# A transformer block on one core: the last gate exponential moved behind the last gelu, and the last tile finished in two halves

## The reference

```python
x = x + attn(layernorm(x))            # 16 heads of 8, causal, with ALiBi slopes
z = layernorm(x)
logits = rms(z @ gate_w.T + gate_b) * rms_w          # 8 experts
g = max(softmax(logits / 0.5));  norm_g = g / (g + 1e-6)
h = gelu(z @ w1[e] + b1[e])           # every expert e, 256 hidden features each
y = sum over e of (h @ w2[e] + b2[e])
out = x + y * norm_g
```

## Time and profile before

| | us |
|---|---|
| median of 3 runs | 312.45 (312.29 to 312.54) |
| the profiled execution | 311.52 |
| its span, first to last instruction | 309.8 |
| PE busy | 283.4 (91%) |
| DVE busy | 206.7 (67%) |
| ACT busy | 187.2 (60%) |
| POOL busy | 90.3 (29%) |

### The profile page before, as it was taken

The page is one execution under the profiler, slowest core; times in us unless marked ns, Lnnn a source line. Parts: engine busy times, 40 slices in busy tenths (PEclk is TensorE's granted clock), DMA queues, the critical chain, the costliest instruction groups (busy, mean ns, idle before and its releaser), DMA issues.

```text
span 309.8 us, 5270 instructions
## 1 busy us (share of the span) xinstructions
PE 283.4 (91%) x1643; PEld 181.9 (59%) x1643; DVE 206.7 (67%) x831; ACT 187.2 (60%) x290; POOL 90.3 (29%) x212
## 2 busy tenths in 40 slices
PE   8527899999779999999999999999999999989993
PEld 3413665655547666757566576666566655647871
DVE  5878668787877767565777784648776821367871
ACT  6480066746539376958467296857397796525462
POOL 1449200713133246021431164020400333500250
PEclk9955789999999999999999999999999999999998
DMA  7441005230300023004000141011001000000101
GB/s 203 160 121 45 4 2 201 51 112 17 108 2 2 0 55 115 0 8 114 0 6 0 38 120 44 2 41 47 3 2 38 0 3 2 0 1 2 34 0 34
DMA packets 12811, 13.47 MB, mean 43 GB/s; under 512 B 2224, under 2 KB 9264, under 8 KB 12528
## 3 DMA queue, kind: packets, MB, share of 16 engines
q1 hardware_dynamic: 11596, 11.89, 12.4%
q0 software_dynamic: 1024, 1.05, 1.6%
q10 hardware_dynamic: 164, 0.21, 0.3%
HBM read 5.40 MB, written 1.05 MB: 21 GB/s over the span
## 4 chain that ended last, share of the span: by engine, by line
PE 61%; DVE 25%; POOL 5%; issue 4%; ACT 2%; DMA 1%; DVEq 0%; POOLq 0%; ACTq 0%
DVE unused L1189 14%; PE ffn_bank L933 11%; PE pv_bank L865 8%; PE v_ring L809 8%; PE a_ring L831 8%; PE a_ring L754 5%; PE a_ring L755 4%; PE a_ring L756 4%; PE a_ring L843 3%; POOL var L375 1%; PE v_ring L816 1%; DVE z L1087 1%; PE v_ring L894 1%; PE v_ring L878 1%; POOL var L376 1%
## 5 line engine op out<-in xcount | busy, mean ns | idle before, releaser
L1189 DVE CUSTOM_DVE_ANT_0 unused<-v_ring,cst 128x256 bf16<-128x256 f32 (+3 forms) x256 | 111.4, 488 | 44.2 <-PE v_ring L809 39.8
L620 ACT ACTIVATE probs<-a_ring 128x512 f32<-128x512 f32 x160 | 86.9, 599 | 70.2 <-PE a_ring L843 40.9
L809 PE MATMUL v_ring<-k_stack,q_stack 128*128 128x512 f32 (+1 forms) x176 | 82.2, 506 | 3.6 <-DVE row_max L1189 1.8
L831 PE MATMUL a_ring<-q_stack,k_stack 128*128 128x512 f32 (+3 forms) x256 | 63.3, 329 | 0.3 <-ACT probs L620 0.3
L638 ACT ACTIVATE hidden<-a_ring,cols_sb 128x512 f32<-128x512 f32 x64 | 43.1, 689 | 27.8 <-PE a_ring L756 27.7
L831 PEld LDWEIGHTS a_ring<-q_stack,k_stack 128*128 128x128 f32 x256 | 45.1, 192 | 13.3 <-issue 5.5
L933 PE MATMUL ffn_bank<-hidden,w_sb 128*128 128x512 f32 x100 | 51.4, 599 | 0.9 <-ACT hidden L638 0.9
L809 PEld LDWEIGHTS v_ring<-k_stack,q_stack 128*128 128x128 f32 x176 | 34.1, 200 | 25.4 <-issue 11.4
L865 PE MATMUL pv_bank<-probs,v_ones 128*32 128x256 f32 (+3 forms) x512 | 42.4, 440 | 0.0
L539 POOL TENSOR_SCALAR_AFFINE_SELECT probs<-probs 128x512 f32<-128x512 f32 x16 | 10.1, 634 | 105.9 <-ACT probs L620 105.9
L754 PE MATMUL a_ring<-zT_hi,w_hi 128*128 128x512 f32 x64 | 28.2, 441 | 0.8 <-DVEq L1073 0.8
(11 more groups left out here) (130 smaller groups left out, 340.6 us busy)
## 6 DMA issues: line engine op xcount, KB each, us to landing
k_stack<-k_hi SPq DMA_DIRECT2D x60, 32.0 KB
q_stack<-q_hi SPq DMA_DIRECT2D x6, 256.0 KB
hidden<-w SPq DMA_DIRECT2D x1, 1024.0 KB, 7.5
k_stack<-k_lo POOLq DMA_DIRECT2D x32, 32.0 KB, 2.1
x_res<-x SPq DMA_DIRECT2D x4, 256.0 KB, 2.8
w_sb<-w SPq DMA_DIRECT2D x1, 1024.0 KB, 7.1
out<-result SPq DMA_DIRECT2D x4, 256.0 KB, 2.2
x_in<-x SPq DMA_DIRECT2D x3, 256.0 KB, 3.1
```

What stands on the lines that cost most here:

```text
L620: act.activation(probs[:, n % 2, quads[0]:quads[-1] + 1, KIND_AT[kind]:KIND_AT[kind] + cols], a_bank()[:, 0:len(quads) * cols].rearrange(" ...
L809: pe.matmul(dst, q_stack[b % 2][:, s, n * P:(n + 1) * P], k_stack[:, s, quads[0]:quads[-1] + 1, 0:cols], start=True, stop=True).then_inc(v ...
L831: last = pe.matmul(dst[:, at:at + P * (TB - j)], k_stack[:, s, q, j * P:(j + 1) * P], q_stack[b % 2][:, s, j * P:T], start=(at == 0), stop ...
L1189: ins = dve.tensor_tensor_reduce(unused[:, (uses[0] - 1) % V_BANKS, at:at + cols], bank_[:, at:at + cols], cst[:, C_MASK + T - cols:C_MASK ...
```

## The change

Three things are done, all in the last batch's end.

The gate's exponential moves on ACT from behind gelu 13 to behind gelu 15. The evacuation of `ffn_bank` is two activations of 128 x 256, each with its own `ffn_evacuated` increment; PE transposes two 128-token tiles after each and puts the halves in two banks of `v_ring`; DVE gates two tiles of each half and raises `result_ready` on the second instruction itself, with no `settle` and no `v_freed`; SP issues a store of 128 KB for each half, and waits for five stores in all instead of four.

```diff
@@ sync
             store(B - 2)
-            store(B - 1)
-            sp.wait_ge(stored, 16 * B)
+            for h in range(2):
+                tiles = slice(h * TB // 2, (h + 1) * TB // 2)
+                sp.wait_ge(result_ready, B + h)
+                sp.dma_start(out_view[B - 1][:, tiles, :], result[:, tiles, :]).then_inc(stored, 16)
+            sp.wait_ge(stored, 16 * (B + 1))
@@ scalar
                 gelu_tile(B - 1, m)
                 if m == 1:
                     evacuate_ffn(B - 2)
-                if m == NT - 3:
-                    gate_exponentials(B - 1)
-            evacuate_ffn(B - 1)
+            gate_exponentials(B - 1)
+            act.wait_ge(ffn2_done, NT * B)
+            act.wait_ge(result_ready, B - 1)
+            for h in range(2):
+                cols = slice(h * T // 2, (h + 1) * T // 2)
+                act.activation(ffn_T[:, cols], ffn_bank[:, cols], ACT.Identity,
+                               bias=b2_sum[:, 0:1]).then_inc(ffn_evacuated, 1)
@@ tensor
-            transpose_ffn(B - 1)
+            for h in range(2):
+                pe.wait_ge(ffn_evacuated, B + h)
+                dst = v_bank()
+                for n in range(h * TB // 2, (h + 1) * TB // 2):
+                    last = pe.transpose(dst[:, n * P:(n + 1) * P], ffn_T[:, n * P:(n + 1) * P], ident)
+                last.then_inc(v_filled, 1)
@@ vector
             route(B - 1)
             take_gates(B - 1)
-            take_ffn(B - 1)
+            dve.wait_ge(stored, 16 * (B - 1))
+            for h in range(2):
+                bank_ = v_bank()
+                for n in range(h * TB // 2, (h + 1) * TB // 2):
+                    ins = dve.scalar_tensor_tensor(out=result[:, n, :], in0=bank_[:, n * P:(n + 1) * P],
+                                                   scalar=gate[(B - 1) % 2][:, n:n + 1], in1=x2[(B - 1) % 2][:, n, :],
+                                                   op0=ALU.mult, op1=ALU.add)
+                ins.then_inc(result_ready, 1)
```

## The result

| | median us | lowest to highest | runs |
|---|---|---|---|
| before | 312.45 | 311.29 to 312.67 | 9 |
| after | 310.18 | 309.08 to 311.36 | 9 |

The ratio is 0.9933, with a 95% interval from 0.9914 to 0.9953: between 1.5 and 2.7 us faster, 2.27 by the medians.

The account below looks back on a forecast made before the run. It took ACT's queue, by the exponential placed in it, to bound the point before the last plain tiles. Gains 1.22 + 0.50 + 0.10 + 0.38 = 2.20 us took the median from 312.45 to 310.25, range 309.8 to 311.3.

Parts of the forecast that it names:

- end of ffn2, from the last split pass: PE's last plain tiles: with the exponential behind gelu 15, ffn2 ends at 303.17 instead of 304.39, gain 1.22.
- ffn2's end to DVE's start: Evacuation and transposes in halves: DVE starts 1.01 behind ffn2 instead of 1.51, gain 0.50.
- DVE's end to SP's last issue: Signal to SP: DVE's instruction raises the semaphore itself, so SP follows 0.07 later instead of 0.17, gain 0.10.
- issue to landing: Last store: half the packets, 1.80 from issue to landing instead of 2.18, gain 0.38.
- the unbroken 1.88: PE's two plain tiles take 1.88 coming straight from other matmuls, not 2.00 with a restart (gain then 1.10).
- The cover: On ACT before the evacuation: 0.86 us left after table load and exponential; without cover the whole 1.5 us on the path.
- The 0.44: A half evacuation on ACT takes 0.44 us, by 0.95 ns a column; bounds 0.34 and 0.68.
- Rival 1: Last stores: the halved store gives nothing back; gain 1.8 or 1.7, time 310.65 to 310.75; chance 0.18.
- Rival 2: ACT becomes the bound before the evacuation: a 2.66 us switch, time 310.85, or another table load, 310.7; chance 0.08.
- Rival 3: TensorE's granted clock falls to 1.2 GHz in the tail: time 312.25, or 313.65 if earlier; chance 0.07.
- Rival 4: Gelu 14 on ACT is held by something else, a bank or ring slot: gain 1.0, time 311.45; chance 0.04.

Follow-up runs that it names:

- e1: Move only, on the kernel before: the exponential behind gelu 15, the end on the whole tile as before; median 310.94 us, ratio to before 0.9953.
- e4: The kernel after with a one-column gelu that nobody reads behind the exponential, bringing one more table load before the evacuation; median 310.63 us.
- e6: The kernel after with evacuation, transposes and gating in four pieces of 128 tokens, each in its own bank, and two stores of 128 KB; median 309.94 us.
- e3: The kernel after with the last tile stored in one piece of 256 KB once both halves are gated; median 310.30 us.
- e7: As e6 (the kernel after in quarters), but with three stores, two by SP and one by ACT's queue, the last of 64 KB; median 310.04 us.
- e5: The kernel after with tiles 14 and 15 of the last batch split by DVE too, `route` ahead of tile 15's split; median 309.49 us.
- e10: The kernel after with 20 unread 128 x 512 bf16 matmuls in PE's idle stretch after batch 0's projections; median 310.10 us, ratio 0.9918.

## Why the prediction was right

It said 310.25 and the runs gave 310.18. Part of that nearness is luck, since the runs of one kernel lie 2.3 us apart: for the profiled execution the same sum said 309.3, and it took 310.28. 0.87 us of that miss lie ahead of the tail. With them taken off, ffn2 ends at 304.06 - 0.87 = 303.19, where the prediction said 303.17. The steps are checked in the tail, each from the rows above.

| step | predicted gain | measured |
|---|---|---|
| end of ffn2, from the last split pass | 1.22 | 3.33 - 2.13 = 1.20 |
| ffn2's end to DVE's start | 0.50 | 1.51 - 1.13 = 0.38 |
| DVE's end to SP's last issue | 0.10 | 0.17 - 0.01 = 0.16 |
| issue to landing | 0.38 | 2.18 - 1.78 = 0.40 |
| sum | 2.20 | 2.14 |

**The exponential's move** was sized right, the choice of the unbroken 1.88 included, and e1 shows it alone. The cover held: 0.88 us of idle ACT where 0.86 was worked out, and 0.94 between gate and gating where 0.77 was. e4 shows what happens when it is used up: 0.53 us on the path.

**The halves** had the right mechanism, but the term of 0.50 was 0.12 too large, by three small pieces of about the same size: a half evacuation took 0.48 on the chain, not 0.44; the pair of transposes 0.45, not 0.41; the step from PE to DVE 0.13, not 0.08. The step from ffn2 to ACT, 0.02 instead of 0.04, gave a little back. The 0.44 came from a line between a 512-column activation with its bias in memory and a 32-column one with none. Those are not the same kind of instruction, contrary to what the prediction said when it took that value. The trace of the kernel before has a 512-column activation that copies a PSUM bank with no bias:

```profile
L628 ACT ACTIVATE y_raw<-pv_bank 128x512 f32<-128x512 f32 x8 | 4.7, 593 | 3.2 <-PE pv_bank L865 3.2
```

It takes 90 ns less than the 683 of the evacuation. From 226 to 593 the slope is 0.76 ns a column, which puts a half at 683 - 256 x 0.76 = 488 ns. The Trainium skill's page "ScalarE: Activation LUTs", section "What ACT_TABLE_LOAD costs", gives 280 ns plus 0.833 ns a column for an activation with such a bias; an estimate by it is 493 ns for 256 columns and 387 for 128. The measured 0.48, and 0.38 on the chain of e6, agree within 0.02. DVE took no time for its new wait: 1.13 in one piece.

**Signal and store** came a little better than forecast. The issue followed DVE's own increment by 0.01 (0.03 in e3), not the 0.07 of the row near 15 us, and e3 shows that 0.4 us of landing goes with the bytes of the last store.

**The rivals.** Rival 1 (the halved store gives nothing) fell: two humps, the second flowing before the first could have landed at about 307.6, and 1.78 in all. Rival 2 (ACT's drain, or a load more) fell in the trace of after, which has one load and none between exponential and evacuation, and e4, with a small gelu beside the load, shows that its milder form would have cost 0.5, where the prediction had 0.4 for the load alone. Rival 3 (the clock falls in the tail) fell: the granted clock is 1.00 until the store's end, and lower only behind it:

```profile
302.00:305.40 3.40, 2.83 (x10) 1.09 (x8) 1.09 (x6) 2.04 (x4) 0.00 (x0) 1.00 0.00 0
305.40:308.10 2.70, 0.01 (x1) 0.00 (x0) 0.91 (x4) 0.00 (x0) 0.00 (x0) 1.00 0.33 97
308.10:308.50 0.40, 0.00 (x0) 0.00 (x0) 0.00 (x0) 0.00 (x0) 0.00 (x0) 0.59 0.00 0
```

Rival 4 (gelu 14 held by something else) fell too: in the trace of after, gelu 14 starts at 299.58, 0.04 behind the end of its ffn1 product (299.14 + 0.40), and gelu 15 0.03 behind the end of its own at 300.94.

What the prediction did not see is the spread of the runs. It took 0.25 us from three of them; nine and more runs show over 2 us for the same kernel.

## What to carry to other kernels

In the last microseconds nothing is hidden, so look there for work of an engine that others wait for behind it: a small instruction that waits for a slow chain, with table loads on both sides, cost 1.2 us merely by its place in the queue, and nothing once it stood where the engine was idle. A chain of whole-tile steps over several engines gets shorter in pieces as long as the slowest engine's total stays the same, and each piece pays its fixed part beside another engine's work. Of the stores only the bytes of the last one count, until the stores follow each other so closely that the bytes flow without a lull, as in e7. For effects of this size compare the stretch behind a common instruction in both traces, since the spread ahead of it can be larger than the change.

## What the runs showed that was not expected

**The start of the kernel decides as much as the change.** Over the experiments the kernel before ran 49 times. Of these runs 47 fall into three groups by the mean granted clock of TensorE, as do the nine of after, and the change is the same 2.1 to 2.3 us between matching groups:

| | highest clock | middle | lowest |
|---|---|---|---|
| before: clock, median span, runs | 0.962 to 0.963: 309.9 (18) | 0.958: 310.7 (13) | 0.953 to 0.954: 311.1 (16) |
| after: clock, median span, runs | 0.966: 307.8 (3) | 0.961: 308.4 (3) | 0.956: 309.0 (3) |

That the groups match in this order is my reading; the spacing of 0.005 in the clock is the same in both. The end of the kernel accounts for the shift of about 0.003 between the rows: before, the clock was at 0.52 over the last 2.8 us, worth 0.004 of the mean, and after, at 0.59 over the last 0.4. The traces show where the clock differs between executions. These are stretches of the kernel before and of the kernel after (columns PE, PEld, DVE, ACT, POOL busy, then PEclk, DMA share, GB/s), the same program there:

```profile
11.00:15.50 4.50, 2.80 (x18) 2.39 (x18) 3.89 (x13) 0.48 (x1) 3.25 (x5) 1.00 0.12 35
...
21.00:30.00 9.00, 7.09 (x15) 3.63 (x14) 7.65 (x31) 2.61 (x5) 8.40 (x9) 0.50 0.25 66
30.00:36.00 6.00, 5.07 (x21) 4.11 (x21) 3.31 (x12) 0.00 (x0) 2.93 (x3) 0.66 0.01 3
```

```profile
11.00:15.50 4.50, 4.50 (x18) 3.82 (x18) 3.60 (x12) 0.73 (x2) 2.91 (x4) 0.62 0.14 47
...
21.00:30.00 9.00, 7.30 (x15) 3.84 (x15) 7.39 (x28) 3.09 (x5) 7.92 (x9) 0.50 0.28 73
30.00:36.00 6.00, 5.02 (x21) 4.39 (x21) 3.02 (x15) 0.00 (x0) 3.39 (x3) 0.57 0.01 3
```

In the profiled execution of after the clock was at its lower level (1.2 GHz) for most of the stretch of the first projections, 4.50 us of PE work where before had 2.80 at 2.4 GHz, and it came back later after 30 us. The 0.87 us ahead of the tail come from both, half and half. PE transposes `row_max` at 30.51 and 43.20 before and at 30.98 and 44.09 after: 0.47 us were lost by the first of these places, and 0.42 more between the two.

Over all the traces the second stretch decides more. From one of these transposes to the other it is 12.24 us in e5, where the clock was 0.74 from 30 to 36 us, and 14.01 in e4, where it was 0.50; e5 has the earliest tail of all (300.57) and e4 the latest (302.55), though the clock was 1.00 in both from 11 to 15.5. Of the 1.98 us between their tails, 1.77 arise there.

**Matmuls at the front of PE's long idle stretch did not keep the clock up behind it.** In both kernels PE idles for over 5 us between the projections of batch 0 and the transposes of batch 1 at about 21 us. Matmuls that nobody reads were put there:

```diff
             project_v(0)
+            idle_products(12)
             transpose_x(1)
```

> The kernel after, with 12 matmuls of 128 x 512 in bf16 whose result nobody reads (as the kernel already has 21 of them at its start) in PE's idle stretch of 5.5 us between the projections of batch 0 and the transposes of batch 1. In the traces the granted clock falls to 0.50 in that stretch and stays there from 21 to 30 us; it is back at 1.00 somewhere between 36 and 45 us, and the time to the tail differs by 1.5 us between executions with it. Theory (the low clock of the start costs time, and comes of that idle stretch): clock above 0.9 from 21 to 45, all up to 3 us less, and the runs lie closer together. Rival (the stretch is not what lowers the clock, or DVE bounds there anyway): span as after, 307.3 to 309.6, and PEclk digits of the start as before. Second rival (the added products run at the low clock, take 0.43 each and delay the transposes): up to 1 us slower.

Measured: median 309.45 (309.09 to 310.54), ratio to before 0.9906 (0.9876 to 0.9935), tail start 300.72, span 307.3. In the idle stretch the clock was 0.92, but from 21 us on it was 0.50 as ever:

```profile
15.50:21.00 5.50, 1.22 (x7) 0.49 (x5) 4.32 (x20) 4.19 (x5) 1.65 (x3) 0.92 0.44 127
21.00:30.00 9.00, 7.01 (x15) 3.54 (x13) 7.73 (x31) 2.53 (x5) 8.48 (x9) 0.50 0.25 66
```

> As with 12, with 20 such matmuls: 4.3 us at full clock, which still fits into the 5.5 us; 8.6 us at the low clock, which does not. Theory: as with 12 or better, since PE is busy until shortly before the transposes. Rival (the clock falls all the same): 3 us slower than after.

Measured: median 310.10 (308.80 to 310.19), ratio 0.9918 (0.9890 to 0.9947), clock 0.94 in the idle stretch and 0.50 again from 21 to 30. The theory's clock above 0.9 did not come, and neither did the 3 us that the rival of e10 set as the price.

But neither kernel kept PE busy up to the transposes. The products ran at once behind the projections, and PE idled again:

```profile
13.66 2.76 PE L769 MATMUL ffn_bank<-unused 128*128 128x512 bf16 x11
20.71 1.11 PE L777 MATMUL v_ring<-cst,xn 128*128 128x128 f32 x4 [4.29 <-DVE xn L1100]
```

In e10 it idled for 2.65 us. In both the clock was still 1.00 from 18.5 to 19.5 us, where before and after had 0.50, and fell between 19.5 and 21, while PE stood. So products placed at the front only moved the fall; whether a PE that works until the transposes keeps its clock was not tried. Whether the 0.7 us by which the first of these medians lies under after's is real stays open, since the intervals overlap and the second shows only 0.1. So does what sets the clock in the projections near 11 us.
